# Two stacked attentions: value products of two key tiles side by side on TensorE, and a fourth buffer of exponentials

## What is computed

```python
# xa: 16 heads of 16; the 1601 context rows are 257 image rows and 1344 text rows,
# with projections and RMS norms of their own
img_x = attention(q, k_img, v_img); txt_x = attention(q, k, v)
x = x + linear(txt_x + img_x, o_w, o_b)
# ca: q = layernorm(x), k = v = context, 16 heads of 16, causal:
# query qi (0..255) sees keys up to qi + 1345, hidden scores are -10000
scores = where(ki <= qi + (Sk - Sq), q k^T / sqrt(16), -10000)
x = x + softmax(scores) v
```

## Time and profile before

| | us |
|---|---|
| three runs | 1924.55, 1930.42, 1940.26 |
| median | 1930.42 |
| span of the profiled execution | 1935.6 |
| stretch from the first to the last scores of `xa` | 649.1 to 1121.4 |
| the same of `ca` | 1519.0 to 1867.0 |

### The profile page before, as it was taken

The page is one execution under the profiler, slowest core; times in us unless marked ns, Lnnn a source line. Parts: engine busy times, 40 slices in busy tenths (PEclk is TensorE's granted clock), DMA queues, the critical chain, the costliest instruction groups (busy, mean ns, idle before and its releaser), DMA issues.

```text
span 1935.6 us, 32748 instructions
## 1 busy us (share of the span) xinstructions
PE 1754.9 (91%) x12374; PEld 1137.1 (59%) x12374; DVE 1274.9 (66%) x2850; ACT 858.6 (44%) x1404; POOL 558.1 (29%) x945
## 2 busy tenths in 40 slices
PE   5999999999877899899899989997888899999988
PEld 4888888888765445455454445664554444444447
DVE  6767676675656777777778543444355688888844
ACT  3343433333342265645646732441232456666652
POOL 5543444443233140320501012441111223331230
PEclk9999999999988799999999979998897999999998
DMA  3000010110006457245264185644602157655100
GB/s 116 27 12 12 23 33 2 33 57 12 18 1 129 88 109 113 39 107 77 38 138 61 15 270 188 214 174 114 132 1 49 35 74 145 82 95 75 18 1 22
DMA packets 91480, 142.74 MB, mean 74 GB/s; under 512 B 14566, under 2 KB 59819, under 8 KB 91324
## 3 DMA queue, kind: packets, MB, share of 16 engines
q1 hardware_dynamic: 86924, 127.79, 31.3%
q10 hardware_dynamic: 2528, 7.74, 1.3%
q0 software_dynamic: 1872, 5.13, 0.7%
HBM read 109.68 MB, written 32.03 MB: 73 GB/s over the span
## 4 chain that ended last, share of the span: by engine, by line
PE 70%; DVE 16%; ACT 5%; issue 4%; POOL 3%; DMA 1%; SPq 0%; ACTq 0%; DVEq 0%; POOLq 0%
PE bank L1235 9%; PE bank L1195 9%; PE bank L1214 8%; PE bank L1956 5%; PE bank L1543 5%; PE bank L1842 3%; PE bank L777 3%; PE bank L1844 3%; PE bank L1843 3%; PE bank L1975 3%; DVE xa_part_max L1308 2%; PE bank L2418 2%; PE bank L2403 2%; PE bank L742 1%; DVE da_neg L2537 1%
## 5 line engine op out<-in xcount | busy, mean ns | idle before, releaser
L1308 DVE TENSOR_REDUCE xa_part_max<-bank 128x1 f32<-128x448 f32 (+1 forms) x512 | 269.9, 567 | 38.9 <-PE bank L1195 35.8
L1269 ACT ACTIVATE xa_e<-bank 128x1024 f32<-128x1024 f32 (+1 forms) x208 | 212.7, 1023 | 138.0 <-PE bank L1214 136.0
L1269 ACT ACTIVATE ca_e<-bank 128x1024 f32<-128x1024 f32 (+2 forms) x208 | 196.4, 957 | 89.1 <-PE bank L1214 88.3
L1308 DVE TENSOR_REDUCE shared<-bank 128x1 f32<-128x400 f32 (+1 forms) x384 | 206.7, 570 | 35.3 <-PE bank L1195 31.4
L1195 PE MATMUL bank<-xa_kst,xa_qst 122*128 122x448 bf16 (+1 forms) x512 | 164.6, 354 | 13.4 <-DVE xa_part_max L1308 8.7
L1235 PE MATMUL bank<-xa_e,xa_vaug 128*17 128x256 f32 (+2 forms) x1792 | 140.0, 387 | 1.6 <-ACT xa_e L1269 0.6
L981 POOL TENSOR_TENSOR gsa_qk<-gsa_qk,gsa_rot 128x512 f32<-128x512 f32 x64 | 81.9, 1280 | 164.7 <-DVE gsa_rot L897 164.7
L1235 PE MATMUL bank<-ca_e,ca_vaug 128*17 128x256 f32 (+2 forms) x1664 | 125.7, 375 | 3.2 <-POOL ca_e L1380 1.4
L1214 PE MATMUL bank<-xa_qst,xa_kst 128*128 128x256 bf16 (+1 forms) x832 | 127.3, 275 | 0.0
L1543 PE MATMUL bank<-xa_wkv,shared 128*128 128x256 f32 (+1 forms) x448 | 120.1, 397 | 7.6 <-SPq L281 3.4
L1195 PEld LDWEIGHTS bank<-xa_kst,xa_qst 122*128 122x128 bf16 x512 | 45.6, 98 | 109.0 <-DVE xa_part_max L1308 64.2
(11 more groups left out here) (402 smaller groups left out, 4223.9 us busy)
## 6 DMA issues: line engine op xcount, KB each, us to landing
xa_kst<-xa_k_parts SPq DMA_DIRECT2D x96, 200.1 KB, 8.1
ca_kst<-ca_k_parts SPq DMA_DIRECT2D x96, 200.1 KB, 8.1
xa_k_parts<-xa_parts SPq DMA_DIRECT2D x8, 1200.8 KB, 6.9
ca_k_parts<-moe_ctx_parts SPq DMA_DIRECT2D x8, 1200.8 KB, 5.7
moe_gu<-in_expert_gate_up SPq DMA_DIRECT2D x8, 1024.0 KB, 14.7
shared<-in_ctxT_split ACTq DMA_DIRECT2D x4, 1601.0 KB, 9.3
moe_ctxT<-in_ctxT SPq DMA_DIRECT2D x8, 800.5 KB, 8.4
ca_cv<-in_ctx SPq DMA_DIRECT2D x4, 1536.0 KB
```

Source lines behind the costliest of these rows:

```text
L1269: e.activation(self.e[m % 3][0:rows, :, first:T], banks[m % 2][0:rows].rearrange("p a (h t) -> p (a h) t", t=T)[:, :, first:T], ACT.Exp, s ...
L1308: e.tensor_reduce(top, work[:, 0:hi - lo], AX.X, ALU.max).then_inc(*reduced(t, *step))
```

## The change

The due time of `pv` is no longer one per tile. At every even tile position k the steps `pv` of tiles k-1 and k are given out together, both 1.7 tile times behind the `exp` of tile k (2.4 if POOL's masking touches one of them); at k = 0 there is only tile 0. So the value products of tiles 1 and 2, 3 and 4, up to 11 and 12 are issued one directly behind the other, the odd one 1.2 tile times later than before. `acc` moves from 0.5 to 0.75 and `fin` from 2.1 to 2.3 tile times behind the unit's end. Both attentions use this.

`Attention` takes further buffers of exponentials (`exps`), and the buffer of tile m is `e[m % len(e)]`. `CA` gets a fourth, laid over `dwk`; `XA` keeps three.

```diff
--- before.py
+++ after.py
@@ -1041,7 +1041,7 @@
 
 
 
-            def __init__(self, ctx, tag, keys, scale, tiles, chunks, sets, masked=False, k_dram=None, q_dram=None, stacks=None, vaug=(), parts=None, qst=(), early=None):
+            def __init__(self, ctx, tag, keys, scale, tiles, chunks, sets, masked=False, k_dram=None, q_dram=None, stacks=None, vaug=(), parts=None, qst=(), early=None, exps=()):
                 self.tag, self.keys, self.scale, self.tiles, self.chunks = tag, keys, scale, tiles, chunks
                 self.sets, self.masked, self.nk = sets, masked, len(tiles)
                 self.AUG = P - 3 * sets
@@ -1060,7 +1060,7 @@
                 self.negf = early("negf", [P, TB, 2, UNIT])
                 self.neg = early("neg", [P, TB, 2, 3, UNIT], BF16)
                 self.negT = [early(f"negT{i}", [2 * 3 * UNIT, TB, P], BF16) for i in range(2)]
-                self.e = [sb(f"e{i}", [P, UNIT, T]) for i in range(3)]
+                self.e = [*(sb(f"e{i}", [P, UNIT, T]) for i in range(3)), *exps]
                 self.accs = [sb(f"accs{i}", [P, BANK]) for i in range(2)]
                 self.rec = sb("rec", [P, 2 * TB, UNIT])
                 self.part_att = sb("part_att", [P, 2 * TB, UNIT, VW])
@@ -1094,10 +1094,14 @@
                 for n in range(B * UNITS):
                     for k in range(self.nk):
                         yield m, ("exp", n, k, m)
-                        yield m + (1.5 if self.shown(k) is None else 2.3), ("pv", n, k, m)
+                        if k % 2 == 0:
+                            pair = range(max(k - 1, 0), k + 1)
+                            behind = 1.7 if all(self.shown(j) is None for j in pair) else 2.4
+                            for j in pair:
+                                yield m + behind, ("pv", n, j, m - k + j)
                         m += 1
-                    yield m + 0.5, ("acc", n)
-                    yield m + 2.1, ("fin", n)
+                    yield m + 0.75, ("acc", n)
+                    yield m + 2.3, ("fin", n)
                     if self.masked:
                         yield m - 3, ("fin_hidden", n)
                     if n % UNITS == UNITS - 1:
@@ -1233,7 +1237,7 @@
                     for (r0, r1, s, first, last) in self.tiles[k][2]:
                         for j in range(UNIT):
                             mm = e.matmul(bank[4][32 * j:32 * j + VW, s * T + lo:(s + 1) * T], vb[r0:r1, v, g * UNIT + j, :],
-                                          self.e[m % 3][r0:r1, j, lo:T], start=first, stop=last, skip_group_check=True)
+                                          self.e[m % len(self.e)][r0:r1, j, lo:T], start=first, stop=last, skip_group_check=True)
                     mm.then_inc(*pv_mm(t, m))
                     if k == self.nk - 1:
                         pv_mm.also(t, n, "all")
@@ -1262,11 +1266,11 @@
                 if kind == "exp":
                     k, m = rest
                     rows = self.tiles[k][1]
-                    if m >= 3:
-                        q.wait_ge(pv_mm, t, m - 3)
+                    if m >= len(self.e):
+                        q.wait_ge(pv_mm, t, m - len(self.e))
                     q.wait_ge(sc_mm, t, m, "scores")
                     first = self.first(k)
-                    e.activation(self.e[m % 3][0:rows, :, first:T], banks[m % 2][0:rows].rearrange("p a (h t) -> p (a h) t", t=T)[:, :, first:T],
+                    e.activation(self.e[m % len(self.e)][0:rows, :, first:T], banks[m % 2][0:rows].rearrange("p a (h t) -> p (a h) t", t=T)[:, :, first:T],
                                  ACT.Exp, scale=self.scale).then_inc(*exp_ready(t, m))
                 elif kind == "neg" and self.masked:
                     if n >= AHEAD:
@@ -1375,7 +1379,7 @@
                     k, m = rest
                     k0, rows = self.tiles[k][0:2]
                     lo, hi = self.first(k), self.shown(k)
-                    part = self.e[m % 3][0:rows, :, lo:hi]
+                    part = self.e[m % len(self.e)][0:rows, :, lo:hi]
                     q.wait_ge(exp_ready, t, m)
                     e.affine_select(part, part, [[0, UNIT], [1, hi - lo]], ALU.is_ge, 0.0, base=CTX - T + lo - k0, channel_multiplier=-1
                                     ).then_inc(*hidden_out(t, m))
@@ -2297,6 +2301,7 @@
 
         ca_qst0 = early("qst0", [P, UNIT, T], BF16)
         ca_qst1 = dwq[:, 0, :].bitcast(BF16).rearrange("p (h t) -> p h t", h=UNIT)
+        ca_exps = dwk.rearrange("p c n -> p (c n)").rearrange("p (h t) -> p h t", h=UNIT)
         ca_pen, ca_floor = early("pen", [P, TB, 400]), early("floor", [P, TB])
         ca_zeros, ca_bias_ready, ca_pen_in = sig("att_ca_zeros"), sig("ca_bias_ready"), landing("ca_pen")
         CA_FIRST = ("load", "max", "neg", "neg_parts", "neg_turn")
@@ -2637,7 +2642,7 @@
         ca_order_of_tiles = [0, 1, 2, 3, 4, 10, 11, 12, 5, 6, 7, 8, 9]
         ca_tiles = [(v * P, P if v < CA_FULL else CA_TAIL, [(0, P if v < CA_FULL else CA_TAIL, 0, i == 0, i == CA_FULL)], v) for i, v in enumerate(ca_order_of_tiles)]
         CA = Attention(ca_ctx, "ca", CTX, HD ** -0.5, ca_tiles, ca_chunks, 1,
-                       masked=True, k_dram=ctx_parts, q_dram=ca_q_dram, stacks=ca_stacks, qst=(ca_qst0, ca_qst1), early=early)
+                       masked=True, k_dram=ctx_parts, q_dram=ca_q_dram, stacks=ca_stacks, qst=(ca_qst0, ca_qst1), early=early, exps=(ca_exps,))
         CA.x_stage = 5
         X_KEYS[5] = lambda n: ("ca", "add", n // TB, n % TB)
         sb = CA.sb
```

## The result

The changed kernel took 1950.53 us (median of 1947.49 to 1950.95), the kernel before, run beside it, 1929.41 us (1924.55 to 1940.26): a ratio of 1.0092, with an interval of 1.0063 to 1.0121. The forecast was 1906.5 us with a range up to 1921. The profiled execution spans 1949.2 us against 1935.6. The lines of `Attention` have moved by four: L1195, L1214, L1235, L1269 and L1308 are now L1199, L1218, L1239, L1273 and L1312.

What follows compares the result with a forecast made beforehand. PE was taken to set the pace, with DVE close behind in ca. Summed: 34.8 + 1.5 - 7 - 1 - 3.5 - 1 = 23.8 us gained, rounded to 24, from 1930.42 to 1906.5 us; range 1890 to 1921.

Steps and rivals of the forecast that it cites:

- The price of a change of width: On PE around value products: each pair drops one way out and one way in, 0.19 us; gross 34.8 us gained.
- Rival (c): In the pairs on PE: the second group's weight loads wait for the first group's end; zero gain, 1930 us; chance 0.07.
- `acc`, `fin` and the fourth buffer at nothing: The later copy of sums and fin stay hidden behind scores and maxima, and ca's extra exponential buffer costs nothing: 0 us.
- The exponentials: PE's waits at value products for ACT and GpSimd shrink with the extra room: 1.5 us gained, range 0 to 3.
- What DVE takes back: PE waits for DVE's max reductions: 7 us lost in ca, 1 in plain xa units, 3.5 in xa's side-work units.
- The side-work units: Seven xa units with the next batch element's work lose half their 1.04 us saving: 3.5 us, between 0 and 7.
- (d): DVE runs dry during each pair, neg_turn and the next unit's scores come late; about zero at worst; chance 0.04.
- the prediction's last sentence: The forecast falls above all if side-work units, a third of the time, shift in ways the plain ones don't.
- The check of the profile: Signs in the profile after: ca units 18.5 to 18.8 us if right; neg_turn waits over 1 us per unit if slower.
- (b): DVE takes over ca (units 18.9 us), xa's side-work units give nothing: 10 to 16 us gained, 1914 to 1920; chance 0.22.

Runs made afterwards that it cites:

- e4: The kernel before with only the due times of acc and fin moved (0.75 for 0.5, 2.3 for 2.1): 1928.37 us, 0.9989 of the kernel before.
- e2: The changed kernel with pairs and later acc and fin in xa alone, ca's fourth buffer kept: 1949.98 us, 1.0048 of the kernel before.
- e5: The kernel before with each DVE reduction of a max product reading only a quarter of its columns: 1905.98 us, 0.9865 of the kernel before.
- e6: The changed kernel with each DVE reduction of a max product reading only a quarter of its columns: 1890.92 us, 0.9786 of the kernel before.
- e8: The changed kernel with odd tiles' scores half a tile earlier, pairs 1.3 or 1.9 tiles behind, acc at 0.4: 1960.01 us, 1.0102 of the kernel before.
- e9: The changed kernel with pairs taken back in xa's units 0, 1, 4, 8 and ca's first unit per batch element: 1936.6 us, 0.9992 of the kernel before.
- e11: The changed kernel with turned keys' work bank freed after ACT's copy, DVE subtracting from SBUF (later key parts wrong): 1954.06 us, 1.0121 of the kernel before.
- e3: The changed kernel with pairs and later acc and fin in ca alone, xa as before: 1948.64 us, 1.0046 of the kernel before.
- e12: The kernel before with turned keys' work bank freed after ACT's copy, DVE subtracting from SBUF (later key parts wrong): 1938.1 us, 1.0033 of the kernel before.

## Why the prediction was wrong

- **The price of a change of width** (0.19 us per pair) was right, a little low: 0.21. Rival (c) is refuted: 16 instructions run through with no gap between the tiles. The rule of the Trainium skill behind it (TensorE: Matmul & The Clock Gate, Part 3), that a weight load overlaps products in flight only with another row group, isn't borne out here: both groups use all 128 rows, and the pair takes 0.99 us, where by that rule the 0.19 us would have stayed, some 1.2.
- **`acc`, `fin` and the fourth buffer at nothing** was right (e4; ca in e2).
- **The exponentials.** 1.5 us were to be gained. In ca the idle time for them, 1.4 and 0.7 us at the largest, is gone from the waits of the stage; in xa it went from 1.6 to 2.3. About right, and small.
- **The step that failed is "What DVE takes back".** Its terms were 1 us for the plain xa units, 3.5 for those with side work, and 7 for ca. In xa's plain units the waits grew by 1.1 us each, not 0.1, and nearly cancel the saving. In ca they grew by 1.6 us a unit in place of 0.45. I compared sums per unit (17.5 us of DVE in 20.1 looked like room enough) and worked out one stretch of ca. What counts is the order in each half microsecond: three banks of 0.57 us are all that DVE can run ahead or behind. Lone value products, one a tile, stood between the maxima and filled PE's time until a bank came free. For the plain xa units e5 and e6 (DVE halved, the whole saving arrives) and e8 (maxima respaced, half of the waits gone) show it; for the plain ca units e5 and e6 show two thirds of it, and e8's spacing gave nothing, so the rest stays open.
- **The side-work units** were to keep half of their saving; instead xa's units 1, 4 and 8, which have most of the `k_turn`, lost 10.4 us, and ca's first units of a batch element 0.8 to 1.6 each. This term, -3.5 us of 1.04 a unit, had the wrong sign: its bound "between 0 and 7" let the waits eat the saving but no more. Yet a wait can grow past the saving, since here the banks go through DVE, ACT and GpSimd in turn (waits at L1199 for `xa_r` 2.2 to 5.7 us in nine places). e9 shows that the pairs in these very units make the loss. What in them makes it so large stays open: not the reductions alone (e6 still loses 3.0 us in unit 4), and not mainly the bank of the turned keys (e11). The count of units was off as well: four of xa's 16 run at 21.1 us, while ten (0 to 5, 7 to 9 and 12), with 353 of its 472 us, carry side work.
- **The clock** was no term of the sum. In xa it cost up to 12.5 us after against 5.5 before, so up to 7.0 of the 9.6 us lost there, and in ca up to 1.7 of 7.2 (last section). The waits come first, and they ate the saving of 18 us; but that xa ended 9.6 us longer, and not 3, is largely the halved clock behind them.
- **The rivals.** (d) had half of the mechanism, DVE dry in the pair and neg_turn late behind it (the waits at neg_turn in ca grew by 7.9 us, those at the max products of both stages by 36), and put its worst at 1.0 us a unit where 1.2 were needed to break even. Measured, the waits grew by 53 us over 30 units, 1.8 us a unit; that this is just the figure it named for a loss of 1% is in part luck, as some of it is the clock's. It added up stalls of one place; they recur at every pair, and add to the chain over the three engines. It got 0.04 of the chance for a wrong reason: "at its worst" was worked out from a plain unit, and most of xa's time is in the others. That is what the prediction's last sentence warned of.
- **The check of the profile** that it gave did decide: neg_turn waits were to stay under 1 us a unit (15.1 us in 16 units, 0.9, double the 7.2 of before), ca units of 18.9 or more with DVE over 94% were to mean (b). They took 19.4, but with DVE at 89%: neither engine is full, and both wait.

## What to carry to other kernels

Before like work is put together to save the change-over between it, ask what each piece covers where it stands. On an engine that issues in order, a piece that needs no buffer is filler for the wait until a buffer comes free; its worth there can be larger than the change-over, and the busy share of the other engine (83% here) doesn't show it. Cost the move at the depth of the ring (here three banks of 0.57 us), take units with side work by themselves with a loss possible beyond the saving, and apply it unit by unit: in eight of 32 it gained 0.3% of the whole.

## What the runs showed of the hardware

**Behind some short waits TensorE's clock was halved.** Timeline of PE of the changed kernel around two waits, and a window behind the second:

```profile
820.42 0.28 PE L1199 MATMUL bank<-xa_kst,xa_qst 122*128 122x257 bf16 x1 [0.92 <-DVE xa_part_max L1312]
820.63 1.71 PE L1239 MATMUL bank<-xa_e,xa_vaug 128*17 128x256 f32 x16
...
928.68 0.28 PE L1199 MATMUL bank<-xa_kst,xa_qst 122*128 122x257 bf16 x1 [1.84 <-DVE xa_part_max L1312]
...
930.00:937.00 7.00, 7.00 (x44) 2.77 (x47) 3.41 (x9) 3.67 (x7) 2.13 (x3) 0.51 0.26 47
```

Behind waits of 1 to 2 us PE runs for some us at a granted clock of 0.51, the lower of its two levels (1.2 GHz of 2.4); the pair at 820.63 is 1.71 us long in place of 1.06. Not every such wait has one behind it: the 1.8 us before unit 4 (at 794 us) had none. xa had two such stretches before and six after, and unit 4's mean clock went from 1.00 to 0.96, unit 8's from 0.99 to 0.93. Half of the time of all halved-clock stretches is what they cost at most, if PE was never idle in them: 5.5 us in xa before and 12.5 after, 8.5 and 10.2 in ca. It goes with the pairs: in xa 12.3 in e2 (pairs there), 5.2 in e3 (none). Part of it falls on units that lost nothing otherwise, such as units 5 and 9. At most 39.1 x 0.04 = 1.6 us of unit 4's 4.2 are the clock's; in e6 the unit lost 3.0 us with its clock at 1.00, so it adds to the loss and isn't its cause. A wait on PE can so cost more than itself, which no term of the sum had.

**A VectorE operation with two SBUF sources can take twice its time beside GpSimd.** The subtraction of 128x256 took 426 ns in the median from SBUF (e12) and 424 from a bank: the source alone changes nothing. But 13 of the 39 from SBUF took 585 to 933 ns, each with a GpSimd operation running when it began, and eight of them ended 0.28 us after it, as here (0.73 us long from 683.56, then the 0.92 us):

```profile
683.56 0.73 POOL L1700 TENSOR_TENSOR xa_kk<-xa_kk,xa_nk 128x256 f32<-128x256 f32 x1
683.64 0.92 DVE L1676 TENSOR_TENSOR xa_r<-xa_wq,xa_parts 128x256 f32<-128x256 f32 x1
```

With a bank as one source none took more than 426 ns (52 in the kernel before), though several began beside such a GpSimd operation. This is where the mean of 529 ns in e12 comes from.
